# A12 of V is split second, G's parts and block sums are read from PSUM, pair 0's x comes by quarters of D, and the last softmax's parts are made before V's

## The reference

```
output = x @ weight;  q = x @ wq;  k = x @ wk
alpha  = q @ k^T                                  (256 x 256 for each graph)
alpha  = max(alpha, 0) * (adj != 0)
alpha  = softmax(alpha, axis=1)                   (over n, the rows)
y      = x + alpha @ output
result = (y - mean(y)) / sqrt(var(y) + 1e-5)      (over the 512 features)
```

## Time and profile before

| | |
|---|---|
| median of 3 runs | 561.83 us (561.16 to 562.45) |
| the profiled execution | 561.95 us |
| its span, first to last instruction | 560.2 us |
| mean granted TensorE clock | 0.988 of full |
| PE busy | 524.3 us (94%), 3816 matmuls |
| DVE busy | 361.4 us (65%), 718 |
| ACT busy | 329.4 us (59%), 783 |
| POOL busy | 282.5 us (50%), 212 |
| DMA | 62.12 MB, q1 busy 31.1% |

### The profile page before, as it was taken

One profiled execution on the slowest core, in us unless ns is written; L12 is line 12 of the kernel. 1 busy time (PEld: TensorE's weight loads), 2 busy tenths in 40 slices (PEclk: granted clock), 3 DMA queues, 4 the chain that ended last, 5 costly groups with the idle time before them and its releaser, 6 DMA issues.

```text
span 560.2 us, 10942 instructions
## 1 busy us (share of the span) xinstructions
PE 524.3 (94%) x3816; PEld 498.3 (89%) x3816; DVE 361.4 (65%) x718; ACT 329.4 (59%) x783; POOL 282.5 (50%) x212
## 2 busy tenths in 40 slices
PE   5995999999999999999999999999999999999994
PEld 4784999999989999998999999899999989999993
DVE  3796565767576576757557675756766575676665
ACT  4652556655655665575566657556665755656453
POOL 0497437447283744727384472738456273844002
PEclk9996999999999999999999999999999999999999
DMA  8304234250523425051332506133250514304011
GB/s 290 160 0 182 82 113 151 73 191 2 189 75 115 149 75 187 0 192 70 125 137 75 187 0 195 67 138 124 75 187 0 203 59 155 107 0 150 2 76 75
DMA packets 23635, 62.12 MB, mean 111 GB/s; under 512 B 1216, under 2 KB 1216, under 8 KB 21696
## 3 DMA queue, kind: packets, MB, share of 16 engines
q1 hardware_dynamic: 23616, 61.87, 31.1%
HBM read 45.09 MB, written 16.78 MB: 110 GB/s over the span
## 4 chain that ended last, share of the span: by engine, by line
PE 78%; DVE 9%; issue 5%; ACT 4%; DMA 2%; SPq 1%; ACTq 0%; POOLq 0%; POOL 0%; DVEq 0%
PE chain L227 10%; PE chain L229 9%; PE chain L228 9%; PE s_bank L227 6%; PE s_bank L228 6%; PE s_bank L229 6%; PE o_bank L227 5%; PE o_bank L228 5%; PE o_bank L229 5%; PE bank_y L228 4%; PE bank_y L229 4%; PE bank_y L227 4%; DVE v_lo L656 3%; ACT v_hi L511 2%; DMA parts<-in_wk_t 2%
## 5 line engine op out<-in xcount | busy, mean ns | idle before, releaser
L892 POOL TENSOR_TENSOR s_lo<-xs,s_hi 128x512 fp32r<-128x512 f32 x60 | 89.9, 1527 | 102.0 <-ACT s_hi L471 102.0
L478 ACT COPY parts<-chain 128x256 f32<-128x256 f32 x180 | 66.9, 372 | 90.2 <-PE chain L229 89.2
L886 POOL TENSOR_TENSOR a_lo<-xt,a_hi 128x512 fp32r<-128x512 f32 x60 | 78.4, 1326 | 56.5 <-ACT a_hi L464 56.5
L227 PE MATMUL s_bank<-t_hi,a_hi 128*128 128x256 f32 x256 | 73.8, 288 | 6.8 <-DVE t_lo L656 6.8
L531 ACT ACTIVATE squares<-xn,neg_mean 128x512 f32<-128x512 f32 x64 | 46.3, 724 | 50.8 <-DVE neg_mean L723 45.1
L228 PE MATMUL s_bank<-t_lo,a_hi 128*128 128x256 f32 x256 | 73.7, 288 | 0.0
L229 PE MATMUL s_bank<-t_hi,a_lo 128*128 128x256 f32 x256 | 73.6, 288 | 0.0
L656 DVE TENSOR_TENSOR v_lo<-parts,v_hi 128x512 fp32r<-128x512 f32 x45 | 49.9, 1111 | 15.7 <-ACT v_hi L511 15.5
L227 PEld LDWEIGHTS s_bank<-t_hi,a_hi 128*128 128x128 f32 x256 | 50.3, 196 | 7.8 <-DVE t_lo L656 7.2
L716 DVE SCALAR_TENSOR_TENSOR xn<-o_bank,xn 128x512 f32<-128x512 f32 x64 | 44.0, 687 | 19.8 <-PE o_bank L229 19.7
L708 DVE SCALAR_TENSOR_TENSOR p_lo<-soft,inv_sum,p_hi 128x256 fp32r<-128x256 f32 x64 | 42.0, 661 | 21.3 <-ACT p_hi L521 21.3
(11 more groups left out here) (173 smaller groups left out, 1741.3 us busy)
## 6 DMA issues: line engine op xcount, KB each, us to landing
xn<-in_x SPq DMA_DIRECT2D x16, 1024.0 KB, 5.3
xt<-in_x_t SPq DMA_DIRECT2D x15, 1024.0 KB, 4.8
out<-xn SPq DMA_DIRECT2D x15, 1024.0 KB, 4.2
adj<-in_adj_t SPq DMA_DIRECT2D x16, 512.0 KB, 3.3
xt<-in_x_t SPq DMA_DIRECT2D x4, 256.0 KB, 4.9
xn<-in_w SPq DMA_DIRECT2D x4, 256.0 KB, 5.0
xn<-in_wq_t SPq DMA_DIRECT2D x1, 1024.0 KB, 8.7
parts<-in_wk_t SPq DMA_DIRECT2D x1, 1024.0 KB, 10.7
```

What stands on the lines that cost most here:

```text
L227: nc.tensor.matmul(dst, a[0], b[0], start=first, stop=False, skip_group_check=shared)
L478: nc.scalar.copy(dst[:, c], src[:, c]).then_inc(copied, 1)
L886: nc.gpsimd.tensor_tensor(a_lo[:, slot, a], xt[:, a], a_hi[:, slot, a].bitcast(F32), ALU.subtract).then_inc(a_lo_ready, 1)
L892: nc.gpsimd.tensor_tensor(s_lo[:, s], xs[:, s], s_hi[:, s].bitcast(F32), ALU.subtract).then_inc(s_lo_ready, 1)
```

## The change

- *V's C12 is split second.* ScalarE's `split_v` order becomes A22, A12, A11, A21, and VectorE's A22, A12, `sum_c21`, A11, A21. TensorE waits for `v_lo_ready` 4p - 2 before P1. VectorE gets a wait for all four `v_lo` ahead of T's `sum_c11`.
- *G.* `g_raw` and its four copies are gone. ScalarE copies only the B12 half (256 columns) of the first two row blocks to `b12`. VectorE takes the `lo` parts from the banks with one operation, (bank x -1) - hi, and makes each block sum in two halves, one operand in a bank, the other in SBUF. TensorE waits for all eight half sums before it writes `o_bank[0]` again. ScalarE casts the last row block of V before W's sums.
- *GpSimd* makes pair 1's `a_lo` and `s_lo` ahead of the sums of W.
- *x of pair 0* is loaded, cast and split by chunks of D, for both graphs and all rows: two pieces of 1 KB for each partition in each of four DMAs. The waits of the first V follow.
- *The last pair's P*: its four parts are made ahead of V's splits, two before A22 and two later, on ScalarE and VectorE.

The diff, cut to its core (the renamed tables and the semaphores' declarations are left out):

```
+        def quarter(x, k):
+            return x[:, k // 2::2, k % 2]
...
-            for k, u in enumerate(A_ORDER):
-                sp.dma_start(xt[:, u], x0[:, u]).then_inc(x0_loaded[k], 16)
+            for k in range(K):
+                sp.dma_start(quarter(xt, k), quarter(x0, k)).then_inc(x0_loaded[k], 16)
...  TensorE
-                    pe.wait_ge(v_lo_ready, 4 * p - 1)
+                    pe.wait_ge(v_lo_ready, 4 * p - 2)
...  fill_first_v
+                    pe.wait_ge(a_hi_ready, k + 1)
                     pe.wait_ge(w_hi_ready, k + 1)
                     for r in range(R - 1):
-                        pe.wait_ge(a_hi_ready, 2 * (k // 2) + r // M + 1)
...  fill_last_of_first_v
+                pe.wait_ge(gt_summed, 8)
...  ScalarE, step
+                else:
+                    split_p(p, 0)
+                    split_p(p, 1)
                 act.wait_ge(o_filled, R * p)
                 split_v(p, A22)
                 if more:
                     split_s(p + 1, S1)
+                else:
+                    split_p(p, 2)
+                    split_p(p, 3)
+                split_v(p, A12)
                 split_v(p, A11)
-                split_v(p, A12)
...  ScalarE, split_g
+                    if j == 0:
+                        act.wait_ge(qk_lo_ready, 2 * K)
+                    nc.scalar.mul(b12[:, j], g_bank[j][:, 1], -1.0).then_inc(b12_copied, 1)
...
-                nc.scalar.mul(g_raw[:, j], g_bank[j][:].rearrange("q j n -> q (j n)"), -1.0).then_inc(g_copied, 1)
...  VectorE, step
                 split_p(p - 1, 2)
+                dve.wait_ge(v_lo_ready, 4 * p)
                 sum_c11(m)
...
+                if not more:
+                    split_p(p, 0)
+                    split_p(p, 1)
                 split_v(p, A22)
-                split_v(p, A11)
                 split_v(p, A12)
                 sum_c21(m)
+                split_v(p, A11)
+                if not more:
+                    split_p(p, 2)
+                    split_p(p, 3)
                 split_v(p, A21)
...  VectorE, split_g
+                def rest_of(dst, rows, hi):
+                    nc.vector.scalar_tensor_tensor(out=dst, in0=rows, scalar=-1.0, in1=hi.bitcast(F32), op0=ALU.mult,
+                                                   op1=ALU.subtract).then_inc(g_lo_ready, 1)
...
+                    dve.wait_ge(b12_copied, j + 1)
+                    rest_of(g_lo[:, b, j], g_bank[j][:, 0], g_hi[:, b, j])
+                    rest_of(p_lo[:, j], g_bank[j][:, 1], p_hi[:, j])
...
-            def sum_gt(b, left, right):
-                nc.vector.tensor_tensor(g_sum(b), left, right, ALU.subtract).then_inc(gt_summed, 1)
+            def sum_gt(b, k):
+                dst = g_sum(b)[:, k]
+                if b == T1:
+                    dve.wait_ge(b12_copied, k + 1)
+                    nc.vector.tensor_tensor(dst, g_bank[k][:, 0], b12[:, k], ALU.add).then_inc(gt_summed, 1)
+                else:
+                    if b != T3:
+                        dve.wait_ge(gt_summed, (1 if b == T2 else 3) + k)
+                    block, less = {T2: (1, g_sum(T1)), T3: (1, b12), D4: (0, g_sum(T2))}[b]
+                    nc.vector.scalar_tensor_tensor(out=dst, in0=g_bank[2 + k][:, block], scalar=-1.0, in1=less[:, k],
+                                                   op0=ALU.mult, op1=ALU.subtract).then_inc(gt_summed, 1)
...  VectorE, order of the start
-            for j in range(K):
+            dve.wait_ge(qk_lo_ready, 2 * K)
+            for j in range(M):
                 split_g(j)
-            sum_gt(T1, raw_block(g_raw, B12), raw_block(g_raw, B11))
-            sum_gt(T2, raw_block(g_raw, B22), g_sum(T1))
-            sum_gt(T3, raw_block(g_raw, B22), raw_block(g_raw, B12))
-            sum_gt(D4, raw_block(g_raw, B21), g_sum(T2))
+                sum_gt(T1, j)
+            for j in range(M, K):
+                split_g(j)
+            for b in (T2, T3, D4):
+                for k in range(M):
+                    sum_gt(b, k)
...  GpSimd
             sum_x(1, first=True)
+            split_a(1, 1)
+            split_s(1)
             nc.gpsimd.tensor_tensor(w_sum(T1), raw_block(w_raw, B12), raw_block(w_raw, B11),
...
-            split_a(1, 1)
-            split_s(1)
```

More of the change, by code:

```diff
@@ L112, in raw_block @@
             return raw[:, 2 * h:2 * h + 2, j * N:(j + 1) * N]
+        b12 = parts[:, 0]
+        def quarter(x, k):
+            return x[:, k // 2::2, k % 2]
         def g_sum(b):
@@ L590, in split_g @@
                     nc.scalar.mul(g_hi[:, b:b + 2, j - 2], g_bank[j][:], -1.0).then_inc(g_hi_ready, 1)
-                if j == 0:
-                    act.wait_ge(qk_lo_ready, 2 * K)
-                nc.scalar.mul(g_raw[:, j], g_bank[j][:].rearrange("q j n -> q (j n)"), -1.0).then_inc(g_copied, 1)
             def split_gt(b):
-                act.wait_ge(gt_summed, b - T1 + 1)
+                act.wait_ge(gt_summed, 2 * (b - T1) + 2)
                 nc.scalar.copy(g_hi[:, G_PLACE[b]], g_sum(b)).then_inc(gt_hi_ready, 1)
@@ L605, in split_first_t @@
                 nc.scalar.copy(t_hi[:, j // 2::2, j % 2], ring[j]).then_inc(t_hi_ready, 1)
-            for k, u in enumerate(A_ORDER):
+            for k in range(K):
                 act.wait_ge(x0_loaded[k], 16)
-                nc.scalar.copy(a_hi[:, 0, u], xt[:, u]).then_inc(a_hi_ready, 1)
+                nc.scalar.copy(quarter(a_hi[:, 0], k), quarter(xt, k)).then_inc(a_hi_ready, 1)
                 act.wait_ge(w_loaded[k], 16)
@@ L633, in _ @@
                 split_first_t(j)
+            split_first_v(R - 1)
             for b in W_ORDER:
                 split_wt(b)
-            split_first_v(R - 1)
             for r in range(R):
                 exponent(0, r)
-            act.wait_ge(gt_summed, 4)
-            act.wait_ge(g_lo_ready, 6)
+            act.wait_ge(gt_summed, 8)
             step(1, 1, first=True)
@@ L647, in _ @@
             step(PAIRS - 1, 1, more=False)
-            for r in range(R):
-                split_p(PAIRS - 1, r)
             for r in range(R):
@@ L671, in sum_c21 @@
                 nc.vector.tensor_tensor(c21, c2, bank_y[:], ALU.add).then_inc(summed, 1)
-            AT = {A22: 1, A11: 2, A12: 3, A21: 4}
+            T_AT, V_AT = {A22: 1, A11: 2, A12: 3, A21: 4}, {A22: 1, A12: 2, A11: 3, A21: 4}
             def split_t(p, u):
-                dve.wait_ge(t_hi_ready, 4 * p + AT[u])
+                dve.wait_ge(t_hi_ready, 4 * p + T_AT[u])
                 whole = {A22: c22, A11: c11, A12: chain_t, A21: c21}[u]
@@ L681, in split_v @@
             def split_v(p, u):
-                dve.wait_ge(v_hi_ready, 4 * p + AT[u])
+                dve.wait_ge(v_hi_ready, 4 * p + V_AT[u])
                 whole = {A22: c22, A11: c11, A12: chain_v, A21: c21}[u]
@@ L734, in normalise, with step @@
                                         ALU.add, ALU.mult).then_inc(normed, 1)
-            def step(p, slot, turn):
+            def step(p, slot, turn, more=True):
                 before = turn if slot == 1 else turn - 1
@@ L798, in split_first_t @@
                 rest(t_lo[:, j // 2::2, j % 2], ring[j], t_hi[:, j // 2::2, j % 2]).then_inc(t_lo_ready, 1)
-            for k, u in enumerate(A_ORDER):
+            for k in range(K):
                 dve.wait_ge(a_hi_ready, k + 1)
-                rest(a_lo[:, 0, u], xt[:, u], a_hi[:, 0, u]).then_inc(a_lo_ready, 1)
+                rest(quarter(a_lo[:, 0], k), quarter(xt, k), quarter(a_hi[:, 0], k)).then_inc(a_lo_ready, 1)
                 dve.wait_ge(w_hi_ready, k + 1)
@@ L838, in _ @@
                 step(2 * i + 2, 0, i + 1)
-            step(PAIRS - 1, 1, PAIRS // 2 - 1)
-            for r in range(R):
-                split_p(PAIRS - 1, r)
+            step(PAIRS - 1, 1, PAIRS // 2 - 1, more=False)
             def mean_of(r):
```

16 lines of the change are left out of this document (4 added, 12 removed).

## The result

The changed kernel takes 541.31 us (median of 4 runs, 540.36 to 542.08) against 561.86: ratio 0.9634, interval 0.9613 to 0.9655. In a later job on another chip the same kernel took 540.22, ratio 0.9605 (0.9586 to 0.9623). The forecast was 536.3 with a range to 540.6: the sign and most of the size are right, 4 to 5 us are missing, and the time lies outside the range. The profiled execution took 540.76 us (span 539.0), against 536.35 in the forecast's own sum.

The account below looks back on a forecast made before the run. TensorE, busy 94%, was taken as the bound, with time to gain only where it waits or runs slowly. 16.3 + 5.8 + 2.35 - 0.4 + 1.55 = 25.6 us off 561.95 gave 536.3, range 534.4 to 540.6.

Parts of the forecast that it names:

- Part 1: V to T in every pair: splitting C12 second removes TensorE's wait before P1, gaining 16.3 us.
- Rival A: V to T: GpSimd holds up A22's split, so the wait goes only in part; 538.1 to 540.9 us, chance 0.09.
- C: Rival, steady part: no gain, P1 or P7 waits as long for `sum_c21` or the first copy; 552.5 us, chance 0.03.
- G's parts and sums from PSUM: Start: parts and half sums at 0.42 us each let S of pair 0 start earlier, gaining 5.8 us.
- the clock stayed at full: Start: with only 1.0 us of idling left TensorE keeps its full clock, gaining 2.35 us more.
- O's cover: Each pair: VectorE's 1.1 us lag is absorbed before O, first two `p_lo` ready by 194.5, O beginning at 197.5.
- rival D: O's first half waits every pair for A11's `v_lo` or the `p_lo` behind; 5 us late gives about 564, chance 0.02.
- the small pieces: Start: loading x in 1 KB pieces makes `wk` land later and shifts the whole start, losing 0.4 us.
- the clock at the end: 3.04 us of idling at the end had not lowered the clock, a reason to take the full clock.
- part 4: Last pair: making the softmax parts ahead of V's splits starts the last O earlier, gaining 1.55 us.

Follow-up runs that it names:

- r3: The changed kernel with the first residual ahead of T's `sum_c21` and the second ahead of A21's split on VectorE; 535.9 us, ratio 0.9528.
- m1: The changed kernel with A12 of V split third again, orders and TensorE's wait as before; 551.97 us, ratio 0.9809.
- b1: The changed kernel with r1's swap, x in 2 KB blocks, and the last pair's A11 split ahead of V's `sum_c21`; 550.42 us, ratio 0.9786.
- b2: The changed kernel with r3's order, x in 2 KB blocks, and the last pair's A11 split ahead of V's `sum_c21`; 534.66 us, ratio 0.9499.
- q1: The changed kernel with A11's split ahead of V's `sum_c21` on VectorE in every pair; 539.6 us, ratio 0.9603.
- m4: The changed kernel with the last pair's four `p_hi` and `p_lo` behind V's splits again; 543.74 us, ratio 0.967.
- r1: The changed kernel with the first residual ahead of T's `sum_c21` on VectorE in every pair; 551.91 us, ratio 0.9821.
- m2: The changed kernel with G copied through SBUF again, GpSimd's new order kept; 546.26 us, ratio 0.9715.

## Why the prediction was right and wrong

*Right.* Part 1's chain to P1 held to a few hundredths: A22's split 0.85, A12's right behind, the wait gone, 16.3 us at that place (O starts 10.08 after T instead of 11.23 to 11.29). Rival A fell: GpSimd didn't hold A22's split longer. The sum and the first copy were in time, against C. G's parts and sums from PSUM are done in 0.42 each (25.43), 0.33 to 0.36 from start to start, where 0.42 was taken, the four splits of the sums took 6.6 (6.8 in the sum), as GpSimd was busy beside them, and S started at 44.82 (forecast: 44.57 with the DMA's 0.4). At 0.8 us of idling the clock stayed at full (1.00 from 43 to 50), as forecast.

*The step that failed* is in part 1: "That lag is paid from O's cover: ... O begins ... at 187.46 + 10.08 = 197.5 and its second half, with the fourth, at 200.3." I gave O's second half one condition, the fourth `p_lo`. It has a second, the semaphore `added`: VectorE must have read each bank in its residual before the bank is written again, and in the kernel before that residual was only 0.3 us early. What makes it late is not VectorE's own lag. That was paid as reckoned: the first two `p_lo` are done 3.1 us before O (406.14; the sum had 3.0), and VectorE idles 0.23 before T's first sum. The delay that I priced at nothing is GpSimd's. Its `s_lo` were checked against P7 to P3, but not its four sums behind them against VectorE: with TensorE's wait gone they end 1.3 us later against O, and VectorE's first `t_lo` takes 1.19 beside the last one instead of 0.68. That puts the residual 0.4 us later, 0.1 too late; with the restart and 0.03 at the second bank it is 0.29 us a pair, the distance of 31.67 from r3's 31.38. The first two such pairs lose 0.43 and 0.33, and in 13 pairs it is 4.0 us. At the last T (the O behind it starts at 504.26) there is no such loss: GpSimd has no sums left, `t_lo` takes 0.69 and the residual starts 1.67 after O's start. In m1 the delay and the loss are both gone, and r3's order of the residuals takes the loss away with `t_lo` as slow as it was. No run moved GpSimd's sums earlier by themselves. It is rival D only in shape (something behind VectorE holds up O); D had a `v_lo` or `p_lo` over 3 us late in it, and these were in time.

*A size that was off:* the small pieces, 0.4 by my sum, cost about 0.7; in the profiled execution G started 0.9 later (19.29 against 18.37). I priced the DMA engines' time per piece (the fixed part comes to 11 ns by my own rates, not 12 to 13, and the 0.4 stays), but the traces point to SP's issue, 0.55 to 0.67 us for each of eight DMAs, W's too, where most took 0.38 to 0.43 with blocks; pieces and issue were not changed separately. The Trainium skill's "DMA: Bandwidth & Descriptors", "Why small descriptors are slow (HBM only)", which gave 0.12, is further off; it prices the transfer alone. *The last O* began 1.61 after V's last matmul ended, 1.49 reckoned: `sum_c21` ahead of A11 is on its path; b1, b2, m1 and q1 take 0.6 of it away.

*A reason that was too good:* the clock at the end. One profile of before with 3.04 us of idling at full clock was taken as a rule. m4 has the same idle and drops to 0.50: there part 4 is worth 1.4 us of waiting and 1.6 of clock (13.2 us from the last O's start to the end, against 11.6 to 11.7 in the others). How often the clock falls at that place isn't shown, since a fall in front of G costs as much. *Together*, in the profiled execution: T(2) starts 7.4 us earlier instead of 7.75, which is 0.3 short, the steady part gives 4.0 back, and the end gains 1.4 instead of 1.55. That is the 4.4 missing.

Left open: how the start's gain divides between PSUM and the new orders of GpSimd and ScalarE; only the first was taken away alone.

## What to carry to other kernels

When a wait of the bound engine goes, all work of the others comes later against it by as much: list every semaphore that the bound engine waits for in the next stage, buffers coming free among them, and write down the margin of each, not only of the data. An engine that makes up its lag (VectorE) can still be slowed by one that doesn't (GpSimd): look at what each instruction with two SBUF inputs now runs beside. A late buffer release shows as a gap too short for the list of waits; look at the distance between like points of two rounds (31.67 against 31.38). When swapping two instructions on an in-order queue, follow both to their last reader: r1 and r3 differ by one more swap and 16 us.

## What the runs showed of the hardware

- The clock after idling did not follow from the idle's length alone. It stayed full after 3.04 us at the end (before) and 2.8 us in front of G (after), and fell after 3.02 us at the end (m4). In front of G it fell in six of the twelve profiles taken after the prediction (b2, r3, r1, m4, m2, m1: idles of 1.8, 2.1, 2.5, 2.9, 3.3 and 4.0 us) and stayed in the others (0.9 to 2.8). From G's first matmul to S's it is 27.2 us with the fall (r3: 18.87 to 46.06) and 25.5 to 25.6 without (after: 19.29 to 44.82): 1.6 us, which goes into the spread of the single runs. Windows of r3, whose G starts at 18.87:

```profile
18.00:20.00 2.00, 1.13 (x5) 0.95 (x6) 2.00 (x5) 2.00 (x5) 0.00 (x0) 1.00 0.98 404
20.00:22.00 2.00, 2.00 (x7) 1.56 (x6) 2.00 (x5) 2.00 (x5) 0.00 (x0) 0.56 0.09 37
22.00:24.00 2.00, 2.00 (x6) 1.54 (x6) 2.00 (x4) 0.07 (x1) 1.35 (x2) 0.59 0.00 0
```

- A DVE instruction of 128x512 with two SBUF inputs beside a busy GpSimd takes 0.85, 0.94, 1.19, 1.5 or 1.8 us by its place against GpSimd's instructions, 0.69 alone; with one input in PSUM 0.67 to 0.69 in every place.
- Splitting the partition's 2 KB into two pieces lengthened SP's issue of that DMA (0.38 to 0.43 us in the kernel before, 0.55 to 0.67 after) and of W's between them (0.42 to 0.50 before, 0.57 to 0.60 after), whose pieces stayed as they were.
